# A spline network in eight written-out steps of 157 columns instead of ten of 125

## The reference, cut to what matters

```
def b_splines(x, grid, k):                       # K = 3, G = 5: 8 values per feature
    x = x[..., None]
    bases = ((x >= grid[:-1]) & (x < grid[1:])).astype(x.dtype)
    for j in range(1, k + 1):
        left = (x - grid[:-(j + 1)]) / (grid[j:-1] - grid[:-(j + 1)])
        right = (grid[j + 1:] - x) / (grid[j + 1:] - grid[1:-j])
        bases = left * bases[..., :-1] + right * bases[..., 1:]
    return bases
def kan_layer(x, grid, w_base, w_spline):
    base = jax.nn.silu(x) @ w_base.T
    spline = jnp.einsum('nig,oig->no', b_splines(x, grid, K), w_spline)
    return base + spline
h = kan_layer(xf, grid, w1_base, w1_spline)      # 1250 x 512 -> 1250 x 256
out = kan_layer(h, grid, w2_base, w2_spline)     # 1250 x 256 -> 1250 x 512
x = x + out                                      # xf is the layernorm of x
```

## Time and profile before

| | us |
|---|---|
| timed executions | 2302.07, 2295.25, 2295.1 |
| median | 2295.25 |
| the profiled execution's own time | 2292.54 |
| its span in the profile | 2290.8 |
| PE busy | 1976.4 (86%) |
| DVE busy | 1355.7 (59%) |
| ACT busy | 1111.4 (49%) |
| mean granted TensorE clock | 0.953 |

### The profile page before, as it was taken

The page is one execution under the profiler, slowest core; times in us unless marked ns, Lnnn a source line. Parts: engine busy times, 40 slices in busy tenths (PEclk is TensorE's granted clock), DMA queues, the critical chain, the costliest instruction groups (busy, mean ns, idle before and its releaser), DMA issues. The chain is left out here.

```text
span 2290.8 us, 37077 instructions
## 1 busy us (share of the span) xinstructions
PE 1976.4 (86%) x10909; PEld 1516.6 (66%) x10909; DVE 1355.7 (59%) x1929; ACT 1111.4 (49%) x1759; POOL 643.4 (28%) x470
## 2 busy tenths in 40 slices
PE   5877799679969999999967769999999975999998
PEld 2555444245557777777756358888768855999997
DVE  6574477446147667776700535545433349999996
ACT  2563466121047667776600136666322226767674
POOL 3000200004734335444366067777200004000000
PEclk8998899898989999999999889999999998999999
DMA  2200870113048778888555157776301130000001
GB/s 92 81 1 1 248 248 12 39 60 129 2 154 295 281 246 301 307 299 291 187 143 170 46 152 187 185 190 181 92 28 33 37 165 1 1 1 1 0 0 46
DMA packets 121601, 282.59 MB, mean 123 GB/s; under 512 B 51616, under 2 KB 58778, under 8 KB 111966
## 3 DMA queue, kind: packets, MB, share of 16 engines
q1 hardware_dynamic: 53646, 189.25, 24.1%
q0 software_dynamic: 67792, 91.34, 14.0%
HBM read 242.05 MB, written 53.89 MB: 129 GB/s over the span
## 5 line engine op out<-in xcount | busy, mean ns | idle before, releaser
L2062 PE MATMUL ps<-ft,kw 128*128 128x125 f32 x2880 | 343.8, 280 | 35.9 <-DVE ft L1987 22.8
L2062 PEld LDWEIGHTS ps<-ft,kw 128*128 128x128 f32 x2880 | 332.2, 194 | 49.6 <-DVE ft L1987 29.0
L1146 POOL DMA_INDIRECT xg<-nrows,idx x128 | 211.2, 1650 | 268.3 <-PE ps L1172 239.0
L1464 POOL DMA_INDIRECT pg<-prows,srcI x170 | 210.0, 1235 | 84.2 <-issue 44.1
L1495 PE MATMUL ps<-ehot,msg 125*128 125x125 f32 x1360 | 164.7, 280 | 22.6 <-ACT ehot L1587 14.9
L1495 PEld LDWEIGHTS ps<-ehot,msg 125*128 125x128 f32 x1360 | 159.0, 195 | 36.8 <-issue 25.7
L2011 ACT ACTIVATE ksq<-ksrc,kn 128x750 f32<-128x750 f32 (+2 forms) x144 | 116.6, 813 | 97.4 <-DVE cube L1970 97.4
L1185 PE MATMUL ps<-wh,xh 128*128 128x512 f32 x364 | 151.6, 417 | 6.5 <-DVE xl L1303 4.8
L1931 POOL COPY ksrc<-nT 128x500 f32<-128x500 f32 (+1 forms) x10 | 10.8, 1075 | 489.9 <-SPq L1922 250.5
L1290 DVE TENSOR_TENSOR wgl<-wexp,wh 128x2048 fp32r<-128x2048 f32 x64 | 146.6, 2291 | 0.3 <-issue 0.3
L1230 ACT ACTIVATE wh<-wexp 128x2048 fp32r<-128x2048 f32 x64 | 122.6, 1918 | 44.4 <-PEq L827 44.4
(11 more groups left out here) (293 smaller groups left out, 4263.2 us busy)
## 6 DMA issues: line engine op xcount, KB each, us to landing
wexp<-wexp_d SPq DMA_DIRECT2D x64, 1024.0 KB
wexp<-wexp_d SPq DMA_DIRECT2D x64, 512.0 KB
yrows<-y SPq DMA_DIRECT2D x91, 256.0 KB
yrows<-nought POOLq DMA_DIRECT2D x1, 16384.0 KB, 56.3
attr<-attr_d SPq DMA_DIRECT2D x42, 250.0 KB
kw<-kw_d SPq DMA_DIRECT2D x2, 4608.0 KB
qs<-qk SPq DMA_DIRECT2D x32, 156.2 KB, 6.6
ks<-qk SPq DMA_DIRECT2D x32, 156.2 KB, 7.2
```

Of the source, the lines that this page charges most:

```text
L1146: pool.indirect_dma_start(xg[:, e % 2, h, :], None, d["nrows"], bass.IndirectOffsetOnAxis(ap=idx[:, 2 * e + h:2 * e + h + 1], axis=0), bou ...
L1464: pool.indirect_dma_start(pg[:, p % 4, t % 2, :], None, d["prows"], bass.IndirectOffsetOnAxis(ap=c.srcI[:, t:t + 1], axis=0)).then_inc(s_g ...
L2062: mm = pe.matmul(out[:, m * B:m * B + B], w[:, k, f, m * P:m * P + P], ft[:, f % RF, a:a + B], start=False, stop=False, skip_group_check=True)
```

## The change

There are now NC = 8 chunks of CB = 157 columns. Since 8 x 157 is 1256, the last chunk begins at column 1093, not 1099, and so computes six columns a second time; `output` leaves these six out of what it adds to `xT` (`fresh`). The buffers are 942 columns wide (628 + 314), and instructions have 628, 942 or 314 columns. There are 10 steps: two of the first layer alone, six full ones, two of the second layer alone.

Four blocks of 157 columns no longer fit into one PSUM bank, so the second layer's sums take two banks a step (2 + 2y and 3 + 2y), each with two blocks, and each bank has its own opening and closing zero matmul. DVE's addition reads both banks in one instruction.

The hardware loop is gone: all ten steps are written out on every engine, addresses and wait values are constants, and the waits for the scaled weights now stand in every step.

The diff, cut to its core (unchanged parts and repeats of `B` to `CB` are left out):

```diff
-        XW, WIDE = KD * B, (KD + KH) * B
+        NC, CB = 8, -(-N // 8)
+        XW, WIDE = KD * CB, (KD + KH) * CB
+        start = lambda t: min(t * CB, N - CB)
...
-        def passes(eng, one, end=NB):
-
-            for t in range(4):
-                one(t, t % 2)
-            with eng.Fori(2, end // 2) as i:
-                for y in range(2):
-                    one(i * 2 + y, y)
-            for t in range(end, NB + 2):
+        def passes(one, end=NC + 2):
+
+            for t in range(end):
                 one(t, t % 2)
...
                     dve.wait_ge(s_sum, t + 1)
-                    to = c.xT[:, :, (t - 2) * B:(t - 1) * B] if fixed(t) else c.xT[:, :, bass.ds((t - 2) * B, B)]
-                    dve.tensor_tensor(to, to, c.ps[:, 2 + y, 0:KD * B].rearrange("p (m n) -> p m n", n=B),
-                                      ALU.add).then_inc(s_o, 1)
+                    fresh = (t - 2) * CB - start(t - 2)
+                    to = c.xT[:, :, start(t - 2) + fresh:start(t - 2) + CB].rearrange("p (c m) n -> p c m n", c=2)
+                    new = c.ps[:, 2 + 2 * y:4 + 2 * y, 0:2 * CB].rearrange("p c (m n) -> p c m n", n=CB)
+                    dve.tensor_tensor(to, to, new[:, :, :, fresh:], ALU.add).then_inc(s_o, 1)
...
-                        layers.append((w2, KH, KD, KD, c.ps[:, 2 + y, 0:KD * B]))
+                        layers.append((w2, KH, KD, KD, 2 + 2 * y))
                         pe.wait_ge(s_o, t)
-                    for *_, out in layers:
-                        pe.matmul(out, c.zero16[0:1, 0:P], c.zero16[0:1, 0:out.shape[1]],
+                    banks = [c.ps[:, bank + i, 0:2 * CB] for _, _, _, M, bank in layers for i in range(M // 2)]
+                    for out in banks:
+                        pe.matmul(out, c.zero16[0:1, 0:P], c.zero16[0:1, 0:2 * CB],
                                   start=True, stop=False, skip_group_check=True)
...
-                        for w, K, first, M, out in layers:
-                            if f and fixed(t):
+                        for w, K, first, M, bank in layers:
+                            if f:
                                 if w is w2:
                                     pe.wait_ge(s_ws2, f)
...
-                                    mm = pe.matmul(out[:, m * B:m * B + B], w[:, k, f, m * P:m * P + P],
-                                                   ft[:, f % RF, a:a + B], start=False, stop=False,
+                                    mm = pe.matmul(c.ps[:, bank + m // 2, m % 2 * CB:m % 2 * CB + CB],
+                                                   w[:, k, f, m * P:m * P + P],
+                                                   ft[:, f % RF, a:a + CB], start=False, stop=False,
                                                    skip_group_check=True)
```

More of the change, by code:

```diff
@@ L1900, in spline_network @@
         kcol = lambda r, i: c.kn[:, r, i:i + 1]
[L1901 to L1903 removed]
+        has_x = lambda t: t < NC
+        has_h = lambda t: t >= 2
         def columns(t):
             return slice(0 if has_x(t) else XW, WIDE if has_h(t) else XW)
[L1908 to L1915 removed]
+        def passes(one, end=NC + 2):
+            for t in range(end):
                 one(t, t % 2)
@@ L1925, in inputs @@
                 def inputs(t, y):
-                    if not fixed(t) or t >= 2:
+                    if t >= 2:
                         pool.wait_ge(s_cube, (t - 1) * NKNOT + 2)
                         pool.wait_ge(s_si, t - 1)
-                    chunk = slice(t * B, t * B + B) if fixed(t) else bass.ds(t * B, B)
-                    pool.tensor_copy(src[:, y, 0:XW].rearrange("p (k n) -> p k n", n=B), c.nT[:, :, chunk])\
+                    pool.tensor_copy(src[:, y, 0:XW].rearrange("p (k n) -> p k n", n=CB),
+                                     c.nT[:, :, start(t):start(t) + CB])\
                         .then_inc(s_x, 1)
@@ L1939, in one @@
                 def one(t, y):
-                    if not fixed(t) or t + 1 < NB:
-                        inputs(t + 1, 1 - y)
-                passes(pool, one, NB - 2)
+                    inputs(t + 1, 1 - y)
+                passes(one, NC - 1)
             @block.vector
@@ L1988, in one @@
                                                  ALU.mult, ALU.max).then_inc(s_ft, 1)
-                        if i == MID and (not fixed(t) or t >= 3):
+                        if i == MID and t >= 3:
                             output(t - 1, 1 - y)
-                passes(dve, one)
-                output(NB + 1, 1)
+                passes(one)
+                output(NC + 1, (NC + 1) % 2)
             @block.scalar
@@ L2024, in one @@
                                 .then_inc(s_r, 1)
-                        if i == MID and (not fixed(t) or 1 <= t <= NB):
+                        if i == MID and 1 <= t <= NC:
                             act.wait_ge(s_sum, t)
-                            act.activation(src[:, 1 - y, XW:WIDE], c.ps[:, 1 - y, 0:KH * B], ACT.Copy)\
+                            act.activation(src[:, 1 - y, XW:WIDE], c.ps[:, 1 - y, 0:KH * CB], ACT.Copy)\
                                 .then_inc(s_h, 1)
-                passes(act, one)
+                passes(one)
             @block.tensor
@@ L2060, in one @@
                                 for k in range(K):
-                                    a = (first + k) * B
-                                    mm = pe.matmul(out[:, m * B:m * B + B], w[:, k, f, m * P:m * P + P],
-                                                   ft[:, f % RF, a:a + B], start=False, stop=False,
+                                    a = (first + k) * CB
+                                    mm = pe.matmul(c.ps[:, bank + m // 2, m % 2 * CB:m % 2 * CB + CB],
+                                                   w[:, k, f, m * P:m * P + P],
+                                                   ft[:, f % RF, a:a + CB], start=False, stop=False,
                                                    skip_group_check=True)
                         mm.then_inc(s_mm, 1)
-                    for *_, out in layers:
-                        mm = pe.matmul(out, c.zero16[0:1, 0:P], c.zero16[0:1, 0:out.shape[1]],
+                    for out in banks:
+                        mm = pe.matmul(out, c.zero16[0:1, 0:P], c.zero16[0:1, 0:2 * CB],
                                        start=False, stop=True, skip_group_check=True)
                     mm.then_inc(s_sum, 1)
-                passes(pe, one)
+                passes(one)
 def finish(c, d):
```

4 lines of the change are left out of this document (2 added, 2 removed).

## The result

Six runs of each kernel give a median of 2284.21 us (2280.65 to 2287.54) for the changed kernel and 2298.27 us (2295.1 to 2302.07) for the kernel before: 14.1 us less, a ratio of 0.9941 with a 95% interval of 0.9927 to 0.9956. The forecast was 12.8 us less and 2282.4; it set out from the 2295.25 us of the first three runs of the kernel before, whose median over six is 3.0 us higher.

What follows compares the result with a forecast made beforehand. DVE was taken to bound all but the last two steps, PE those. Terms - 20.0 + 0.7 + 6.4 + 0.1 = - 12.8 us, from 2295.25 to 2282.4 us; 8-in-10 range 2276 to 2290.

Steps and rivals of the forecast that it cites:

- DVE sets the pace of steps 0 to 7: Steps before the last two: DVE's full-step slot takes 4.45 us against PE's 4.26, so PE stays the faster.
- 20.0 us less on DVE: DVE's steps 0 to 7 sum to 324.4 us instead of 344.4, partly from 72 fewer instructions.
- The loop's 5.1 us: Full steps: writing out the hardware loop saves 0.85 us in each of six steps, if registers cost it.
- Nothing for two banks: DVE's addition to xT: column price only, + 0.13 us for 128 more columns, no extra charge for a second bank.
- The fixed part of a DVE instruction, 0.13 and not 0.157 us: DVE's slots: 0.13 us fixed per instruction from the rows; 72 fewer save 9.4 us, against 11.3 by the skill's page.
- PE's end, + 7.2 us: After DVE's steps: + 0.7 us for PE's last full-step slot, + 6.4 for its two last steps, + 0.1 last addition.
- PE did not take over: Rival for full steps: PE's slot of 4.55 us exceeds DVE's 4.45, giving 2285 us; chance 0.07.
- the loop's time did not stay: Rival for full steps: written-out steps cost as in the loop, 5 x 0.85 us come back, 2286.7 us; chance 0.08.
- the clock's low stretch in full steps: Rival: PE's clock drops repeatedly in full steps; one step wholly at low clock gives 2315 us; chance 0.05.
- The third rival: Clock falls in steps 0 and 1: + 3 and + 8 us, 2293 us, no change; chance 0.08.
- The 0.1 us that the prediction charged PE for a wait in the middle of a slot: PE's full-step slots: the first matmul after a wait costs at most 0.1 us, 1.6 us a step, covered by slack.

Runs made afterwards that it cites:

- The six-chunk kernel: Six chunks of 209 columns instead of eight, with five cube slots and klf, krt written in place; stage 369.2 us, ratio 0.9913 to the kernel before.
- the smaller buffers: Changed kernel, still eight chunks, with five cube slots and klf, krt written in place: stage 374.8 us, one run 2261.09 against 2275.92 us before.

## Why the prediction was right, point by point

**DVE sets the pace of steps 0 to 7.** Shown from both sides: 2.4 us more of PE's work in a full step change nothing, and less work on DVE shortens it down to PE's 39.7.

**20.0 us less on DVE.** Measured 20.9 (344.4 to 323.5). Each step was within 0.2 us: 35.6, 30.4, 42.5, three of 43.2 and two of 42.7, for 35.8, 30.5, 42.6, and 43.3 or 42.8. The straight line through the earlier trace rows held at 628 and 942 columns.

**The loop's 5.1 us.** Measured 5.2 by itself, nearly all of it between `krt` and `ft`.

**Nothing for two banks.** Measured 0.1 us by itself. The longer addition takes 0.80 us for 628 columns, the 0.13 more that the column price gave. The rule of the Trainium skill that the prediction cites, of a clock that swings when PE idles briefly while it cycles through PSUM banks, does not show here: the granted clock was 1.00 over 280 us with two banks alone, and over the last 293.5 us of the stage in the changed kernel.

**The fixed part of a DVE instruction, 0.13 and not 0.157 us.** The slots of 3.14 and 4.44 us fit the rows; with the constant that the Trainium skill gives ("VectorE: DVE Perf Modes", section "The TRN2 errata") as the fixed part, 4 x (0.157 + 942/960) would be 4.55. That formula is for the duration of one instruction, and there the trace is close to it: `klf` takes 0.81 us at 628 columns and 1.13 at 942, where it gives 0.811 and 1.139 (`ft` takes 0.87 and 1.20). In the chain the next one can start before the last has ended: a `krt` of 942 columns starts 1.05 us after a `klf` of 1.13.

**PE's end, + 7.2 us.** Measured from the first cube of the first step with the second layer alone to the last addition's end: 2276.72 - 2230.51 = 46.2 against 2281.37 - 2242.66 = 38.7, so + 7.5. A matmul of 157 columns takes 0.134 us, where I took 0.133.

**The rivals.** PE did not take over, the loop's time did not stay, and the clock's low stretch in full steps was 3.4 us instead of the 6.8 before. The third rival did not come either: the granted clock was 1.00 from 1917.6 to 1978.8 us, which is most of step 0 and all of step 1. The six-chunk kernel has 3.4 us of low clock in the middle of step 0, and they cost DVE nothing; low clock throughout a step was seen in no run, so that rival's price stays untested.

**What was off** is small: 12.8 us were forecast for the stage and 13.3 came, 0.9 more from DVE and 0.3 less at PE's end; the medians have 14.1, and the 0.8 between is within their scatter. The 0.1 us that the prediction charged PE for a wait in the middle of a slot is not paid where PE runs behind, so PE's slot with more work was 4.55 and not 4.68 us; this moved nothing, as PE does not set these steps. What the prediction did not see is how much two profiled executions differ outside of the stage: theirs are 5.1 us apart.

## What to carry to other kernels

Where a chain of vector instructions sets the pace, fit a line through their start-to-start times at two or three widths in the profile; the fixed part times the number of instructions saved is the gain of wider chunks, and the steps at the end, where another engine sets the pace and every column is paid at its rate, are the price. Add up only instructions on the pacing engine, and test by giving the other engine more work: here PE was 96% busy and still had room. If the stages ahead scatter by about as much as the change is worth, compare the stage and not the whole.

## What the runs showed of the hardware that was not expected

- POOL's scaling of 1024 columns stretches DVE instructions that run beside it, about one for each scaling that falls into step 0: four `ft` of 0.87 us take 1.53 to 1.61 and two cubes 1.43 and 1.73, 3.3 us in all. Only that one is stretched, by 0.7 us; the others that run during the same scaling, which lasts 2.8 to 3.8 us, keep their length. A scaling takes 3.46 us on average beside DVE's 628 columns and 3.19 beside 500. The copy of `ksrc` stretches a `krt` of 942 columns from 1.13 to 1.65 us.
- A stage of 375 us repeats within 0.1 us from execution to execution and from chip to chip (374.82, 374.74 and, with the smaller buffers, 374.76), while the start of it moved by 12 us on one chip.
- The fp32 matmul's cadence was 0.1117 us at 125 columns, 0.134 at 157 and (25.78 - 3.10)/128 = 0.177 at 209, the last from this row of the six-chunk kernel and the one of 16 above:

```profile
2187.15 25.78 PE L2060 MATMUL ps<-ft,kw 128*128 128x209 f32 x144
```

From 157 on that is two cycles of 2.4 GHz a column and 0.003 us.
